# Retention layer: constant loads on four semaphores, an early activation table, and another order of the second norm and the chunks in a step

## What is computed

```python
xn = _ln(x, norm1_w, norm1_b)
q, k, v = xn @ wq + bq, xn @ wk + bk, xn @ wv + bv      # 16 heads of 16
gamma = 1.0 - exp2(-5.0 - arange(H))
Dmat = where(diff >= 0, exp(log(gamma) * diff), 0.0)     # diff = query - key
ret = einsum('bhnm,bhmd->bhnd', (q k^T) * hd ** (-0.5) * Dmat, v)
gn = (ret - mu) / sqrt(var + EPS) * gn_w + gn_b          # per head
h = silu(xn @ wg + bg) * gn @ wo + bo
x = x + h
u, g = split(_ln(x, norm2_w, norm2_b) @ w_in + b_in, 2)  # 682 hidden
return x + (silu(u) * g @ w_out + b_out)
# outside: x = _layernorm(x_before + this)
```

## Time and profile before

| | |
|---|---|
| median of 3 runs | 1876.62 us (1875.46 to 1883.51) |
| the profiled execution | 1877.84 us, span 1876.0 us |
| TensorE, matmuls | 1631.2 us busy (87%) |
| TensorE, weight loads | 1280.3 us (68%) |
| VectorE | 1210.7 us (65%) |
| ScalarE | 676.7 us (36%) |
| GpSimd | 272.1 us (15%) |

### The profile page before, as it was taken

How to read it: one execution, slowest core, us unless ns; L and a number is a source line. 1 busy time by engine, 2 the same in 40 slices (tenths; PEclk the granted TensorE clock), 3 DMA queues, 4 the chain that set the end, 5 groups by cost and what they waited for, 6 DMA issues and landing times. The chain is left out here.

```text
span 1876.0 us, 38522 instructions
## 1 busy us (share of the span) xinstructions
PE 1631.2 (87%) x14742; PEld 1280.3 (68%) x14742; DVE 1210.7 (65%) x3881; ACT 676.7 (36%) x1408; POOL 272.1 (15%) x240
## 2 busy tenths in 40 slices
PE   5789997899997678888888677498899999999998
PEld 4577775666655556677776556386688788878876
DVE  2555565455554735566666439627989889888894
ACT  2333332245556246556665333014223222222210
POOL 1344344200000100000000004301001000100000
PEclk9899998999999878999999877599999999999999
DMA  3100000000010278989898450242000000000000
GB/s 122 46 18 18 17 12 18 12 19 25 30 53 29 92 264 308 317 294 327 313 324 316 138 143 18 80 202 91 1 2 13 13 2 13 13 2 13 2 7 13
DMA packets 96469, 175.32 MB, mean 93 GB/s; under 512 B 16032, under 2 KB 80800, under 8 KB 91552
## 3 DMA queue, kind: packets, MB, share of 16 engines
q1 hardware_dynamic: 96288, 172.85, 26.6%
HBM read 93.01 MB, written 79.69 MB: 92 GB/s over the span
## 5 line engine op out<-in xcount | busy, mean ns | idle before, releaser
L104 PE MATMUL bank<-per_xT,per_down 128*128 128x256 f32 x1024 | 250.1, 389 | 2.3 <-ACT per_xT L2380 1.6
L2683 PE MATMUL bank<-per_up,per_act_w 128*128 128x256 f32 x1024 | 242.4, 382 | 0.0
L2683 PEld LDWEIGHTS bank<-per_up,per_act_w 128*128 128x128 f32 x1024 | 195.1, 191 | 26.8
L104 PEld LDWEIGHTS bank<-per_xT,per_down 128*128 128x128 f32 x1024 | 190.2, 192 | 29.9 <-issue 2.7
L2387 ACT ACTIVATE per_act_w<-bank 128x512 f32<-128x512 f32 x128 | 76.2, 597 | 362.9 <-PE bank L104 328.3
L1488 ACT ACTIVATE rel_probs<-rel_summed,rel_low 128x256 f32<-128x256 f32 x256 | 117.2, 518 | 25.7 <-DVE rel_low L1572 25.7
L1572 DVE CUSTOM_DVE_ANT_0 rel_summed<-bank,rel_bias 128x256 f32<-128x256 f32 x256 | 95.0, 419 | 34.6 <-DMA rel_bias<-rel_qr_rows 17.3
L104 PE MATMUL bank<-ret_x2T,ret_w_in 128*128 128x256 f32 x384 | 96.7, 410 | 16.5 <-DVE ret_x2T L442 16.5
L900 DVE TENSOR_REDUCE xat_mx<-bank 128x2 f32<-128x512 f32 x128 | 79.5, 684 | 32.9 <-PE bank L948 32.9
L104 PEld LDWEIGHTS bank<-ret_x2T,ret_w_in 128*128 128x128 f32 x384 | 77.4, 206 | 30.7 <-DVE ret_x2T L442 11.6
L1707 PE MATMUL bank<-rel_band_k,rel_qT 32*128 32x191 f32 x512 | 63.2, 369 | 31.2 <-DVE rel_low L1572 24.0
(11 more groups left out here) (354 smaller groups left out, 3190.9 us busy)
## 6 DMA issues: line engine op xcount, KB each, us to landing
rel_qr_rows<-rel_qr SPq DMA_DIRECT2D x32, 1024.0 KB, 8.5
rel_p_rows<-rel_probs SPq DMA_DIRECT2D x32, 1024.0 KB, 6.7
rel_bias<-rel_qr_rows SPq DMA_DIRECT2D x64, 384.0 KB, 4.4
rel_by_dist<-rel_p_rows SPq DMA_DIRECT2D x64, 384.0 KB, 4.5
per_down<-in_per_down SPq DMA_DIRECT2D x1, 4096.0 KB, 24.8
per_up<-in_per_up SPq DMA_DIRECT2D x1, 4096.0 KB, 12.6
ret_xin<-in_x SPq DMA_DIRECT2D x8, 256.0 KB, 2.8
xat_cT<-in_contextT SPq DMA_DIRECT2D x8, 256.0 KB, 2.8
```

Source lines behind the costliest of these rows:

```text
L104: last = pe.matmul(dst, wt[:, c], src[:, c, :], start=c == 0, stop=c == DC - 1)
L2683: last = pe.matmul(tiles(bank[7])[:, t, :], act_w[:, n % 2, k, t * P:t * P + P], up[:, k, :], start=k == 0, stop=k == COLS - 1)
```

## The change

The loads are issued in another order and counted on four semaphores: the identity; `cols` and `own`; wq and wk; and wv, wg, rows, fade, seen, gn_eps. Each engine waits for a group where it first needs it. ScalarE executes one small Silu on `bq_own` before its first step. In the fourth step of a period TensorE does v and gate before the transposes of `gated`. In the first step it does the second-norm transposes right behind `down`, into ring bank 2 instead of 0, and the second half of `turn_values` behind `values`, waiting there for x2T, which frees that bank. VectorE computes x2T right behind the sum, then s1 and cen, and the statistics of y last. The chunks use the ring in the order 0, 1, 2, 0, 1, 0, and the waits that guard the banks are changed to fit.

```diff
-    loads = [(ident[:], ident_in), (cols[:], w["cols"]), (wq[:], w["wq"]), (own[:], w["own"]), (wk[:], w["wk"]),
-             (rows[:], w["rows"].partition_broadcast(P)), (wv[:], w["wv"]), (wg[:], w["wg"]),
-             (fade[:], w["fade"]), (gn_eps[:], w["gn_eps"]), (seen[:], w["seen"])]
+    loads = [(cols[:], w["cols"]), (own[:], w["own"])]
+    qk_loads = [(wq[:], w["wq"]), (wk[:], w["wk"])]
+    vg_loads = [(wv[:], w["wv"]), (wg[:], w["wg"]), (rows[:], w["rows"].partition_broadcast(P)),
+                (fade[:], w["fade"]), (seen[:], w["seen"]), (gn_eps[:], w["gn_eps"])]
-    CHUNK_RING = (1, 2, 0, 1, 0, 1)
+    CHUNK_RING = (0, 1, 2, 0, 1, 0)
@@ sync
         sp.dma_start(xin[:, 0], batch_of(x_in, 0)).then_inc(x_loaded[0], 16)
+        sp.dma_start(ident[:], ident_in).then_inc(ident_loaded, 16)
         load_all(sp, loaded, loads)
+        load_all(sp, qk_loaded, qk_loads)
+        load_all(sp, vg_loaded, vg_loads)
@@ gpsimd, vg_of(s)
+                if b == 0:
+                    pool.wait_ge(vg_loaded, 16 * len(vg_loads))
@@ scalar
         act.wait_ge(loaded, 16 * len(loads))
         act.wait_ge(consts, 1)
+        nc.scalar.activation(su[:, 0, 0:4], bq_own[:].rearrange("p a c -> p (a c)"), ACT.Silu)
@@ vector
                 dve.tensor_tensor(yout[:, b % 2], tiles(ring[0]), x_x1[:, b % 2], ALU.add).then_inc(sum_ready, 1)
-                dve.drain()
-                row_stats(dve, yout[:, b % 2], st[:, 2], mv[:, 2, b % 2], ve[:, 2, b % 2]).then_inc(var3, 1)
+            if (b := norm2_of(s)) is not None:
+                dve.wait_ge(turned2, b + 1)
+                if b >= 2:
+                    dve.wait_ge(uv_mm, HC * (b - 1))
+                for c in range(DC):
+                    last = dve.tensor_scalar(x2T[:, b % 2, c, :], tiles(ring[2])[:, c, :], n2w[:, c:c + 1],
+                                             n2b[:, c:c + 1], ALU.mult, ALU.add)
+                last.then_inc(x2T_ready, 1)
             if (b := turn_of(s)) is not None:
...
                 last.then_inc(cen_ready, 1)
-            if (b := norm2_of(s)) is not None:
...
+            if (b := down_of(s)) is not None:
+                dve.drain()
+                row_stats(dve, yout[:, b % 2], st[:, 2], mv[:, 2, b % 2], ve[:, 2, b % 2]).then_inc(var3, 1)
...
             if (b := vg_of(s)) is not None:
+                if b == 0:
+                    dve.wait_ge(vg_loaded, 16 * len(vg_loads))
@@ tensor
-        pe.wait_ge(loaded, 16 * len(loads))
+        pe.wait_ge(ident_loaded, 16)
@@ turn_values, t == 1
                 pe.wait_ge(v_ready, min(m + 1, nb))
+                if m >= 2:
+                    pe.wait_ge(x2T_ready, m - 1)
@@ turn_second
             pe.wait_ge(xhat2_ready, b + 1)
-            pe.wait_ge(g_biased, min(m + 1, nb))
-            if m >= 3:
-                pe.wait_ge(sum_ready, m - 2)
-            turn(pe, tiles(ring[0]), xhat2[:, b % 2], ident).then_inc(turned2, 1)
+            pe.wait_ge(v_ready, min(m + 1, nb))
+            turn(pe, tiles(ring[2]), xhat2[:, b % 2], ident).then_inc(turned2, 1)
@@ chunk
             if c == 0:
                 pe.wait_ge(x2T_ready, b + 1)
+                pe.wait_ge(g_biased, min(m + 1, nb))
+                if m >= 3:
+                    pe.wait_ge(sum_ready, m - 2)
+            if c == 1:
                 pe.wait_ge(cen_ready, min(m, nb))
             if c >= 3:
-                pe.wait_ge(h_ready, HC * b + (0, 0, 0, 1, 3, 4)[c])
+                pe.wait_ge(h_ready, HC * b + (0, 0, 0, 1, 2, 4)[c])
@@ turn_first
             if m >= 2:
-                pe.wait_ge(h_ready, HC * (m - 2) + 2)
+                pe.wait_ge(h_ready, HC * (m - 2) + 3)
@@ queries_keys
-            if m >= 0:
-                pe.wait_ge(g_biased, m + 1)
-            if m >= 2:
-                pe.wait_ge(h_ready, HC * (m - 2) + 5)
+            if b == 0:
+                pe.wait_ge(qk_loaded, 16 * len(qk_loads))
             for wt, to, done in ((wq, ring[2], q_mm), (wk, ring[0], k_mm)):
+                if done is k_mm and m >= 0:
+                    pe.wait_ge(g_biased, m + 1)
+                if done is k_mm and m >= 2:
+                    pe.wait_ge(h_ready, HC * (m - 1))
@@ values_gate
+            if b == 0:
+                pe.wait_ge(vg_loaded, 16 * len(vg_loads))
@@ order of a step
             if (b := down_of(s)) is not None:
                 down(b, m)
+            if (b := norm2_of(s)) is not None:
+                turn_second(b, m)
             if (b := turn_of(s)) is not None:
                 turn_values(b, 0, m)
-                turn_values(b, 1, m)
...
                 chunk(b, 5, m)
+            if (b := vg_of(s)) is not None:
+                values_gate(b)
             if (b := out_of(s)) is not None:
...
                 turn_gated(b, m)
-            if (b := vg_of(s)) is not None:
-                values_gate(b)
             if (U := unit(s)) is not None:
                 values(U)
-            if (b := norm2_of(s)) is not None:
-                turn_second(b, m)
+            if (b := turn_of(s)) is not None:
+                turn_values(b, 1, m)
```

More of the change, by code:

```diff
@@ L183, in retention_layer @@
     mv, ve, rs = sb("mv", [3, 2, TT, 2]), sb("ve", [3, 2, 2]), sb("rs", [3, 2, 2])
-    loaded, late, consts = sem("loaded"), sem("late"), sem("consts")
+    ident_loaded, loaded, qk_loaded, vg_loaded = sem("ident_loaded"), sem("loaded"), sem("qk_loaded"), sem("vg_loaded")
+    late, consts = sem("late"), sem("consts")
     x_loaded, stored = [sem(f"x_loaded{k}") for k in range(XS)], [sem(f"stored{u}") for u in range(2)]
```

## The result

The changed kernel takes 1865.81 us (median of 18 runs, 1858.16 to 1874.63) where the kernel before takes 1880.47 (18 runs beside them). The ratio is 0.9929, with a 95% interval of 0.9915 to 0.9943: 13.3 us faster (10.7 to 16.0). The forecast was 19.7 us faster. TensorE's busy time fell by 3.4 us only, so some three quarters of the gain is waiting that went away. The forecast's absolute time, 1856.9, started from the first three runs of the kernel before (1876.62); the 18 runs beside the change are at 1880.47, so 3.9 us between the forecast time and the measured one are the base.

A forecast was written before the change was run, and what follows sets the result against it. TensorE's waits in the retention layer, some 310 of 1876 us, were taken as the bound. Terms summed to 23.1 us, less 3.4 for the clock: 19.7 faster, 1858.1 from 1877.84, median 1856.9; range 1849 to 1866 (0.87).

The forecast's parts named there:

- Start: Layer's start: transposes wait only for their own load, and the table load leaves q's copies; 7.1 us gained.
- Steps 4 to 6: Step 4's second half of the value transposes follows `values`, delaying s1, cen and step 5's masks: −1.1 us.
- Step 7: values/gate first removes the 2.51 us wait for `gated` and the 1.59 us fallen clock behind it: +4.1 us.
- Steps 8 and 9: The second norm's reordering gains 1.6 us, with no y to normalise behind it.
- A period: Steps 12 to 28: 1.5 of 3.3 us kept after a new wait before `values`, plus 0.45 in the fourth step: 1.95.
- −3.4 for the clock: Clock falls behind the new wait before `values`, two of five steps taken, at 1.69 us each; bounds 0 and 8.45.
- Tail: Step 32 on: GpSimd's set-up is later, delaying ScalarE, but chunks 0 to 2 run earlier; +1.0 us, bounds 0.7 and 2.4.
- a new wait as long as the old: Rival: y's chain on VectorE takes 1.5 us more, periods keep only 0.45 each; 9.4 us gained, 1867; chance 0.09.
- y meeting GpSimd's power: Rival: y's normalisation on VectorE meets GpSimd's 5.43 us power of s3; 12.5 us slower, 1889; chance 0.04.
- the case of five falls: Rival: the clock falls every time in the new wait before `values`; 14.7 us gained, 1862; chance 0.15.
- a start that gives nothing: Rival: the queue's order, not the semaphore, sets when loads land; 12.6 us gained, 1864; chance 0.05.
- the signs of being wrong: q and k start after 10, the wait at `values` is over 2.5 us or absent, or periods stay above 39.5.

The follow-up runs named there:

- The start alone: Kernel before with only the four semaphores, the new load order and the early Silu: ratio 0.9937, −11.8 us.
- the change without the start: Changed kernel with its loads and early Silu undone, all reordering kept: ratio 0.9987 to the kernel before, −2.4 us.
- the second norm's order alone: Kernel before with only the moved second-norm and value transposes, VectorE's new order and the new chunk ring: ratio 1.0010, +1.9 us.
- values/gate first alone: Kernel before with only values/gate moved ahead of the transposes of `gated`: ratio 0.9955, −8.5 us.
- the kernel with the start and values/gate first: Changed kernel with the second norm's order and chunk ring as before: ratio 0.9906 to the kernel before, −17.7 us.
- The three kernels whose pause at `values` is closed: Changed kernel with y's normalisation behind the masks (0.9890), with chunk 2 ahead of `values` (0.9859), or with both and the early set-up (0.9836).
- the set-up issued early: Changed kernel with GpSimd's set-up of the next layer ahead of y's root in step 32: ratio 0.9878 to the kernel before, −22.9 us.

## Why the forecast was half right

**Start, forecast 7.1.** Measured 7.4 at values/gate, with every time of the working within 0.3 us: transposes at 6.70 (6.6), values/gate at 14.85 (15.1), one load before 8. Neither later wait binds. Right, and also on why. How long q and k take differs between executions with the same start (5.24 to 6.78 us), and values/gate with it (14.59 to 15.55).

**Steps 4 to 6, forecast −1.1.** Measured −0.5 up to step 6, and −2.3 more within it. There q and k took 5.41 us (53.80 in the changed kernel) where they had taken 3.72 (60.10 before): a clock fall that the forecast didn't have. The start alone has it too (53.16, 5.17), but so has the change without the start (61.13, 6.01) and the second norm's order alone (62.32, 5.00); values/gate first alone has none. So neither part alone is its cause, and why it falls there stays open. What failed is that the forecast has a clock term for the chunk pairs only, and lets a gain pass unchanged through all other stages.

**Step 7, forecast 4.1.** Measured 4.2 (4.6 to 8.8). The number is right, and in part by luck: with the fall at q and k of step 6 TensorE comes to step 7 later, and the start alone then does the step in 8.52 us, the changed kernel in 7.67. So of the 4.2 only 0.9 is left to values/gate first; the rest undoes the loss in step 6. **Steps 8 and 9, forecast 1.6.** Measured 0.8. The step that failed: the forecast took the gain of a later period over, but the kernel before has no wait for x2T in step 9. The six of the earlier trace rows are those of steps 13, 17, 21, 25, 29 and 33, and chunk 0 at 87.25 follows the scores without a pause. Measured up to chunk 0, 0.2 us is gained, and 0.6 are chunks 0 and 1 at a higher clock (3.72 us for 4.35). **Step 11, forecast 0.45.** Measured 0.6.

**A period, forecast 1.95 each, and −3.4 for the clock.** The mechanism was right in each part, and `values` came 15.70 us behind the scores of step 16 as worked out (170.35 less 154.65): no wait for x2T, a new wait of 1.78 to 2.15 at `values` for the masks, for y's normalisation in front of them, and two falls in five steps (17 and 29). From step 12 to step 31 5.9 us were forecast and 4.6 came. The term that was mis-sized is the 1.7 us for the clock, which is nearly all of the 1.5 kept: it was credited in every period, where the kernel before loses it in four of five chunk pairs, not in step 25, which the earlier trace rows had shown. Falls went from four to two, which is 3.1 us (5.13 − 3.72 + 3 x 1.69 less 2 x 1.69) and not 8.45 − 3.4 = 5.1. Of the 4.6 the clock is thus two thirds, by luck of where falls come; the second norm's order itself gives next to nothing: the 15.70 us (142.74 to 158.44) were 15.81 (235.26 to 251.07) in the one period of before that had no fall, from step 24 on. The experiment with that order alone says the same: 0.2 us up to step 31.

**Tail, forecast +1.0, bounds 0.7 and 2.4.** Measured −3.9, outside both bounds, and the largest miss, 4.9 us. This is the step of the forecast that failed. The row was read right: the memset moved behind cen and the statistics. The forecast let ScalarE wait for it, and TensorE start chunks 0 to 2 without it. But TensorE's own list enters the next layer at step 32, and among its first waits there is one for the same set-up. The profile before put TensorE's 6.10 us of waiting to x2T, and x2T did end later than the set-up there (0.75 us later, at 324.01, held up itself by the memset, below):

```profile
323.02 0.99 DVE L442 TENSOR_SCALAR ret_x2T<-bank,ret_cols 128x256 f32<-128x256 f32 x2
323.06 0.20 POOL L812 TENSOR_TENSOR xat_bq_own<-xat_cols,xat_scale_own 128x4 f32<-128x4 f32 x1
```

A wait on two things was shown here as a wait for the later. Once x2T came early, the other stood alone, and the profile showed it as "issue", with no releaser. From `down` to chunk 0 took 13.4 us before and 16.3 after; 0.7 more was lost ahead of `down`, where `values` and the transposes of step 31 ran slower, and 0.2 in chunks 0 to 3. The list of what is queued behind the moved root was made for GpSimd and ScalarE, and not for TensorE.

**Step 36, forecast 0.65.** Measured 0.9.

**The rivals.** The range's condition for the lower gains, a start that isn't earlier, didn't come, nor did a new wait as long as the old or y meeting GpSimd's power. The result of 13.3 us is near the case of five falls (14.7) and near that of a start that gives nothing (12.6) in size, and neither is its cause: there were two falls, and the start gave its 7.4. Of the signs of being wrong only one came, and for one period: q and k start at 8.95, the wait at `values` is there and under 2.5 us, and of four periods one (39.77) is over 39.5. None of the signs looked at the tail. Start +0.3, steps 4 to 9 −2.4, periods −1.3, tail −4.9, step 36 and step 11 +0.4 are −7.9, from 19.7 to 11.8 by step 37; the two executions differ by 12.7.

**What stays open.** The layers that weren't edited, from the channel mix to the end, take between 1282.8 and 1292.8 us in the profiled executions of these kernels, with no order that follows the edits. So the ends of single traces say little, and stages are compared by their starts within the edited layer. The channel mix starts 14.1 us earlier in the changed kernel (579.1 for 593.2, `mix_r`), near the 13.3 of the runs; the 2.3 us between that and the 11.8 arise behind step 36, in the mixed end and the second layer, and aren't explained here. Open is also what decides where the clock falls, and so how the 4.6 us of the periods would repeat in another execution.

## What to carry to other kernels

When a step is moved on one engine, look up every wait of every engine for what is queued behind it, also the waits that are satisfied today: a wait for two things was shown as one for the later, and the other was the next bound. Removing a pause in front of one stage by moving work to the stage behind gains only if the engine that prepares the next stage's input (here VectorE) comes free earlier too; put what nobody is waiting for (y's normalisation) behind what TensorE waits for. And count a clock fall only in the periods in which the rows show one, and don't count on it to go with a pause that is only moved: behind the moved pause it fell in four, two, two, two and one of five steps in the five kernels that have it, and where the pause was closed, in none of five in three kernels.

## What the runs showed of the hardware

**The clock after pauses of nearly the same length.** After 1.95 us of idleness the 16 matmuls took 5.41 us in steps 17, 21 and 29 of the kernel before, after 2.27 in step 25 they took 3.72. In the changed kernel pauses of 1.78 us were followed by a fall in step 17 and by none in step 21:

```profile
198.20 0.86 PE L544 MATMUL bank<-first_shared 128*32 128x256 f32 x16 [1.78 <-ACT first_shared L351]
198.99 3.72 PE L104 MATMUL bank<-ret_x2T,ret_w_in 128*128 128x256 f32 x16
```

And after the 2.15 of step 13, shown above, chunks 2 and 3 took 3.72 too. So in these rows the length of a pause doesn't decide alone. The three kernels whose pause at `values` is closed had no fall at the chunks of any of the five steps.

**A memset on GpSimd holds up VectorE.** The scaling of s1, 128x32 elements, takes 0.18 us in the changed kernel (`ret_s` at 306.11). In the kernel with the start and values/gate first it began with the memset of the next layer's set-up:

```profile
304.38 2.74 DVE L438 TENSOR_SCALAR ret_s<-ret_s 128x32 f32<-128x32 f32 x1
...
304.43 2.66 POOL L819 MEMSET first_shared<- 128x3072 f32 x1
```

In the kernel before it is the same, 2.73 us at 319.53, so there cen and x2T of step 32 came 2.6 us late for it. The Trainium skill ("SBUF — State Buffer", Who interferes with whom) lets a tensor_scalar use the port pair that VectorE and GpSimd share, and the one that comes second waits out the whole instruction of the other. The length agrees. The start times alone don't show the order: both pairs of rows have VectorE 0.05 us ahead of the memset, and yet it was VectorE that waited. With the set-up issued early the two lie apart: the memset stands from 303.30 to 305.96 (rows above), the scaling starts at 305.24, inside it, and ends at 305.98 with it (0.74 us for 0.18). The tensor_reduce of 128x256 that VectorE ran in the middle of that memset (303.85) took 0.42 us, as without one.
